# Last layer of a graph network: gathered rows turned ahead of made rows on TensorE, VectorE's step in another order

## What is computed

```python
x = concatenate([nodes[senders], nodes[receivers], edges], axis=-1)
h = relu(x @ msg_W1 + msg_b1)
messages = relu(h @ msg_W2 + msg_b2)
agg = segment_sum(messages, receivers, num_segments=3125)
y = relu(concatenate([nodes, agg], axis=-1) @ node_W1 + node_b1)
y = y @ node_W2 + node_b2
y = (y - mean(y)) * rsqrt(var(y) + 1e-5) * ln_scale + ln_offset
return nodes + y
```

## Time and profile before

| | |
|---|---|
| median of 3 runs | 1332.59 us (1330.99 to 1334.54) |
| the profiled execution | 1327.6 us, its span 1325.8 us |
| busy, share of the span | PE 76%, DVE 63%, POOL 45%, ACT 34% |
| last layer's loop and what surrounds it | about 716 to 1326 us |

### The profile page before, as it was taken

How to read it: one execution, slowest core, us unless ns; L and a number is a source line. 1 busy time by engine, 2 the same in 40 slices (tenths; PEclk the granted TensorE clock), 3 DMA queues, 4 the chain that set the end, 5 groups by cost and what they waited for, 6 DMA issues and landing times.

```text
span 1325.8 us, 24512 instructions
## 1 busy us (share of the span) xinstructions
PE 1006.6 (76%) x6145; PEld 618.1 (47%) x6145; DVE 830.9 (63%) x2605; ACT 452.6 (34%) x1035; POOL 592.2 (45%) x763
## 2 busy tenths in 40 slices
PE   3788887996667767667696787777787878777685
PEld 2566553553444545445355444434444534444443
DVE  8988877357645556757657554565555555555556
ACT  3677771011434333334013232232232323222232
POOL 6533330000665666654003656555555555555550
PEclk9677778998887788877797899999888998999997
DMA  2000006001111111100523533333333333333331
GB/s 54 2 0 0 0 0 243 1 1 22 24 23 19 20 21 22 21 19 17 168 63 75 138 81 79 76 76 76 77 73 77 75 71 77 75 73 78 72 75 34
DMA packets 145110, 72.80 MB, mean 55 GB/s; under 512 B 111917, under 2 KB 136698, under 8 KB 144922
## 3 DMA queue, kind: packets, MB, share of 16 engines
q1 hardware_dynamic: 127224, 54.98, 16.0%
q0 software_dynamic: 16448, 16.88, 6.9%
q10 hardware_dynamic: 1378, 0.22, 0.1%
HBM read 59.66 MB, written 12.35 MB: 54 GB/s over the span
## 4 chain that ended last, share of the span: by engine, by line
PE 41%; another core or an unknown queue 20%; issue 16%; DVE 12%; ACT 6%; DVEq 2%; POOL 1%; ACTq 1%; DMA 1%; SPq 1%; POOLq 0%
PE seg L1628 10%; PE big L1658 5%; PE big L1552 4%; PE seg L1683 4%; PE seg L1755 3%; PE big L1791 3%; PE seg L1802 2%; ACT A L1345 2%; PE seg L1566 2%; PE big L1781 1%; ACT A L1466 1%; PE seg L1696 1%; ACT A L1472 1%; PE seg L1823 1%
## 5 line engine op out<-in xcount | busy, mean ns | idle before, releaser
L1221 POOL DMA_INDIRECT A<-table,idx x338 | 327.3, 968 | 260.6 <-ACT idx L1317 154.2
L1221 POOL DMA_INDIRECT pair<-table,idx x176 | 176.2, 1001 | 126.8 <-ACT idx L1317 65.0
L1755 PE MATMUL seg<-A 128*128 128x384 f16 (+1 forms) x624 | 137.6, 370 | 44.5 <-issue 19.1
L1466 ACT COPY A<-big 128x512 f32<-128x512 f32 x104 | 61.1, 587 | 249.7 <-remote 156.7
L1345 ACT CAST A<-big 128x500 f32 x208 | 125.4, 603 | 48.0 <-PE big L1557 25.9
L1791 PE MATMUL big<-A 128*128 128x512 f32 x208 | 114.1, 631 | 33.6 <-ACT A L1466 28.3
L2033 DVE COPY A<-seg 128x512 f32<-128x512 f32 x52 | 36.0, 691 | 162.3 <-remote 150.6
L1683 PE MATMUL seg<-A,cur 128*64 128x160 f32 x750 | 94.8, 353 | 46.0 <-issue 45.9
L1397 ACT COPY A<-big 128x500 f32<-128x500 f32 x120 | 66.5, 576 | 181.4 <-remote 113.8
L1755 PEld LDWEIGHTS seg<-A 128*128 128x128 f16 x624 | 60.3, 106 | 140.5 <-issue 91.0
L1658 PE MATMUL big<-A 128*128 128x300 bf16 x480 | 106.1, 367 | 18.8 <-issue 10.4
(11 more groups left out here) (307 smaller groups left out, 1809.6 us busy)
## 6 DMA issues: line engine op xcount, KB each, us to landing
A<-in_edge_attr_dram SPq DMA_DIRECT2D x103, 128.0 KB
A<-drel_flat SPq DMA_DIRECT2D x104, 126.0 KB
spilled_adjacency<-A SPq DMA_DIRECT2D x1, 7074.0 KB, 21.8
A<-spilled_adjacency SPq DMA_DIRECT2D x6, 1152.0 KB, 11.8
A<-table,idx POOLq DMA_INDIRECT x338
A<-pr_table SPq DMA_DIRECT2D x104, 31.5 KB
pair<-table,idx POOLq DMA_INDIRECT x176
A<-low_flat SPq DMA_DIRECT2D x78, 32.0 KB
```

Of the source, the lines that this page charges most:

```text
L1221: pool.indirect_dma_start(out=row(q, j), out_offset=None, in_=table, in_offset=bass.IndirectOffsetOnAxis(ap=idx[:, q, j:j + 1], axis=0)).t ...
L1466: nc.scalar.copy(x_t[:, r, :], big[:, r, :]).then_inc(x_t_ready[r], 1)
L1755: op = nc.tensor.matmul(made[:, 0:held.shape[2] * D], hot_low[:, u, m, :], held[:, k, :, :], start=(m == 0 and k == 0), stop=(m == 3 and k ...
```

## The change

Three things. On TensorE `turn_rows` of the step's lag-1 group stands ahead of `make_rows`. On VectorE the list begins with `choose_rows` and `add_windows` instead of ending with them. And the six instructions that centre `node_w2` and `node_b2` are no longer ahead of the loop, but at the beginning of step 4; `steps` has a new argument for that.

```diff
-        def steps(eng, stages, between=lambda s: None):
+        def steps(eng, stages, between=lambda s: None, ahead=lambda s: None):
...
             for s in range(peeled * Q):
+                ahead(s)
                 one_step(0, s, 0, GROUPS)
...
-            steps(pe, [(0, make_rows), (1, turn_rows), (0, node_hidden), (6, window_sums), (2, hidden_sums), (4, turn_messages), (3, message_sums)])
+            steps(pe, [(1, turn_rows), (0, make_rows), (0, node_hidden), (6, window_sums), (2, hidden_sums), (4, turn_messages), (3, message_sums)])
...
-            for weights, many in ((nw2_sb, HID), (nb2_bc, P)):
-                link(dve.tensor_reduce(st_a[0:many, 0:1], weights, AX.X, ALU.add))
-                link(dve.tensor_scalar(st_c[0:many, 0:1], st_a[0:many, 0:1], 1.0 / D, None, ALU.mult))
-                link(dve.tensor_scalar(weights, weights, st_c[0:many, 0:1], None, ALU.subtract))
-            dve.sem_inc(ev("node_weights_ready"), 1)
-            steps(dve, [(1, receivers), (5, message), (0, senders), (4, plain_hots), (0, node_norm),
-                        (7, add_windows),
-                        (0, choose_rows)],
-                  between)
+            def centre_weights(s):
+                if s != Q:
+                    return
+                for weights, many in ((nw2_sb, HID), (nb2_bc, P)):
+                    link(dve.tensor_reduce(st_a[0:many, 0:1], weights, AX.X, ALU.add))
+                    link(dve.tensor_scalar(st_c[0:many, 0:1], st_a[0:many, 0:1], 1.0 / D, None, ALU.mult))
+                    link(dve.tensor_scalar(weights, weights, st_c[0:many, 0:1], None, ALU.subtract))
+                dve.sem_inc(ev("node_weights_ready"), 1)
+
+            steps(dve, [(0, choose_rows), (7, add_windows), (1, receivers), (5, message), (0, senders), (4, plain_hots), (0, node_norm)],
+                  between, centre_weights)
```

## The result

The changed kernel takes 1370.45 us (median of 4 runs, 1367.82 to 1373.35) against 1331.79 us (4 runs, 1329.96 to 1334.54) for the kernel before on the same chip: 1.0289 times, 95% interval 1.0261 to 1.0317. It is 39 us slower. The forecast of 1326 us and its range up to 1354 us were wrong, and the time lies in the slower rival's span of 1354 to 1383 us.

What follows compares the result with a forecast made beforehand. GpSimd's timeline (gathers, gaps and waits for index copies) was taken to bound the last layer. The early turn's 6.7 us off 1327.6 gave 1320.9; with 5.0 us from execution to median, 1325.9, say 1326 us, range 1312 to 1354.

Steps and rivals of the forecast that it cites:

- slower rival: VectorE becomes the bound: make_rows(3)'s increment held, choosing only at the release, turn and hidden_sums late; 1354 to 1383 us, chance 0.26.
- VectorE, order: VectorE's list with choose_rows first: make_rows(3) and hidden_sums(1) start 0.7 to 1.2 us later, all hidden, costing nothing.
- cover of 2.4 us: Slack between hidden_sums(1) ending at 1008.30 and its use at 1010.72, claimed to hide the later make_rows(3).
- TensorE, the early turn: turn_rows ahead of make_rows on TensorE: copy_rows(0) done early, hidden starts at the release; 6.7 us gained, 0 to 9.4.
- The copy of q = 0: ScalarE's copy_rows(0), predicted within 2 us of the start of each run of six gathers.
- 25.5 us of L1791's waits: TensorE's 14 waits for ScalarE's late copy, predicted to be nearly gone.
- The 6.7 us: Gain claimed for the early turn: 0.48 us off each of 14 pauses before runs of seven gathers.
- price per pause: 0.48 us (953.77 to 954.25) saved per long GpSimd pause by taking copy_rows from in front of hidden.
- increments at that point are prompt: TensorE's turn ending soon after a run's first gather reaches ScalarE at once, so copy_rows(0) is done by 1014 or so.
- price per microsecond: In the slower rival, each microsecond over the cover costs 21 us, once a round.
- Centring: node_w2 and node_b2 centring moved to step 4: first senders 1.65 us earlier, hidden by pr_table loads; nothing, 1.65 us either way.
- Gathers under VectorE's work: senders moving against GpSimd's gathers: no change taken; at worst 0.49 us for each of 63 senders, 31 us.

Runs made afterwards that it cites:

- e17: Changed kernel with senders directly behind choose_rows in VectorE's list: 1331.01 us, 1.0093 times the kernel before.
- e6: Changed kernel with senders ahead of choose_rows at the head of VectorE's list: 1.0071 times the kernel before.
- e2: Kernel before with only VectorE's list of the change (choose_rows and add_windows first): 1.0026 times the kernel before.
- e1: Kernel before with only TensorE's list of the change (turn_rows ahead of make_rows): 1327.38 us, 1.0072 times the kernel before.
- e5: Changed kernel (both new lists) with the centring left ahead of the loop: 1342.24 us, 1.0179 times the kernel before.
- e9: Kernel before with ScalarE's list reordered so that the index copy stands ahead of hidden: 1316.91 us, 0.9993 times the kernel before.
- e7: The changed kernel unedited, measured again beside other runs: 1.0223 times the kernel before.
- e8: Kernel before with TensorE's list beginning turn_rows, hidden_sums, make_rows: 1361.27 us, 1.0326 times the kernel before.
- e13: Changed kernel with an iota between the gathers of q = 0 and 1 and of q = 2 and 3: 1376.69 us, 1.0347 times the kernel before.
- e3: Kernel before with only the centring of node_w2 and node_b2 moved to step 4: 1.0040 times the kernel before.
- e11: Changed kernel with ScalarE's index copy ahead of hidden: 1349.76 us, 1.0225 times the kernel before.
- e12: Kernel before with an iota between the gathers of q = 0 and 1 and of q = 2 and 3: single run, 1303.99 us against 1319.99.
- e16: Kernel before with an iota only between the gathers of q = 0 and 1: 1327.52 us, 0.9954 times the kernel before.
- e14: Kernel before with an iota between the gathers of q = 0 and 1 and of q = 2 and 3, timed: 1335.25 us, 1.0039 times.
- e18: Kernel before with an iota between the gathers of q = 0 and 1 and ScalarE's index copy ahead of hidden: 1311.16 us, 0.9931 times.

## Why the prediction was wrong, step by step

**The step that failed** is "VectorE, order", and in it: "make_rows(3) starts 0.7 to 1.2 us later ... All this is hidden, so it costs nothing". I worked the new chain out from the release of one half and held it against one cover of 2.4 us. But the piece from the end of a choosing to the next make_rows comes back twice a round: 1.4 us behind q = 1 (939.82 to 941.24) and 2.3 us behind q = 2 (944.48 to 946.78), in the round shown and in the median round from 820 to 1297 us, where it was 0.25 and 0.06 us before (behind q = 3 it is near 6 us in both kernels). With senders second it is 1.2 and 0.8 us (e17), with senders first 0.75 and 0.77 (e6), and more than half of the loss is gone. The step was also costed with make_rows still ahead of the turn. That is what e2 measures: its pieces are as long as the changed kernel's (1.5 and 2.35 us), and they are nearly hidden, 0.3%. **Behind the early turn they aren't**: from e1 (1.0072) to e5 (1.0179) the same list costs 1.1%, some 14 us, where I had put nothing.

**TensorE, the early turn.** The copy of q = 0 came early as forecast, and the 25.5 us of L1791's waits went. The 6.7 us didn't come; e1 lost 9 us (1327.38 against 1318.45). I had costed what the turn no longer stands behind, and not what now stands behind the turn: make_rows and with it the choosing, which waits for a held increment once a round (121.4 us in e1, 110.1 in the changed kernel; neither the kernel before nor e2 has such a wait in this stretch), and then the turn itself, 3.1 us in the round shown. That this wait is the price of the early turn isn't shown: e9, with the turn at its old place, has more of it (150.2 us, 36 times, 820 to 1280 us) and is as fast as the kernel before. The price per pause was wrong too: e9 took `hidden` out of every pause and gained 0.1%, with an interval from 0.3% faster to 0.2% slower. And the rows didn't bear out that increments at that point are prompt: the turn of 1014.18 is over at 1014.79, and its copy_rows starts at 1017.48, 2.7 us later and before the last gather (1019.11) was begun.

**Both together** cost more than their sum (1.8% against 0.7 + 0.3), which the runs show and I didn't consider at all. A chain fits the timelines: choosing, turn, make_rows held behind senders, choosing again, with hidden_sums and so the index copy behind it. That this chain is why the two don't simply add is argued, not shown. What the traces do show is where the time goes. Over the whole loop GpSimd waits for indices 59, 60 and 60 times in the three kernels with both lists and ScalarE's list as it was (changed, e5, e7), and 48 to 51 times in the kernel before, e1, e2, e6 and e17. `hidden` waits 144 to 165 us for a named, late hidden_sums in the first three, and 17 to 63 us in the others. e8 is slow in another way, with 51 waits of 3.7 us each.

**The slower rival** named the place (the increment of make_rows of q = 3, the choosing at the release, turn and hidden_sums behind) and the price (1354 to 1383 us), and had 0.26. In the changed kernel's timeline it is there word for word. As the cause it is half right: shorter runs of gathers (e13) didn't take the loss away, and where `hidden` waits longer than before, it is for a hidden_sums that ends late by itself. Its price per microsecond was taken for the 21 rounds of the stretch, where the loop has 26; at 26 the span would be 1359 to 1395 us, and the measured time lies in that too.

**Centring**: I took nothing, with 1.65 us either way. The start moved by nothing that can be told; e3 gives 0 to 0.8%, e5 beside e7 nothing to 1%, so whether some 5 us belong to it remains open. **Gathers under VectorE's work**: no change was right, 950 ns after 970; the lengthening that the Trainium skill (SBUF — State Buffer, SBUF: two separate sides) would have for senders at the start of a run isn't in the mean here. The reverse is in e13, where senders took 1.6 to 2.2 us, 0.73 being usual, 15 times of 78, each time with the iota of a stop begun inside it. **The tail** of 7.6 us more I hadn't looked at: once no gather is left only the chain of the other engines remains, and it is the longer one; that this makes the 7.6 us was not tried.

Still open: why the changed kernel is 2.9% slower on one chip and 2.2% on another, why the early turn alone costs 0.7%, and what part of the loss the pattern of runs makes by itself (seven, three and three in the round shown). e11, with both lists and ScalarE's new one, has only 51 waits for indices and is still 2.2% slower; there each takes 3.6 us.

## What to carry to other kernels

When a stage moves in a list, cost what will stand behind it, not only what it no longer stands behind; and follow the loop that goes from engine to engine over a single buffer (choose, make, choose) through all its turns in a round before calling a delay hidden. Two edits that each lean on the other's old order must be costed together. A producer of the next item (senders) belongs ahead of the step that waits for the present one.

## What the runs showed of the hardware

Many increments that TensorE makes late in a run of gathers reach other engines only about 2 to 2.7 us after the last gather of that run was begun: make_rows over at 948.31, the last gather begun at 949.27, the choosing started at 952.00. An iota of 1.1 us between two gathers also let them through, 1.9 to 2.0 us after the gather ahead of it was begun, 24 times in e12, and the next gathers didn't stop what had been let go. One such stop in a round made the kernel 0.5% faster (e16), two made it 0.4% slower (e14). With ScalarE's new list as well (e18) it is 0.6% under e9. Not every increment in a run is held: in the run of 941.80 the choosing of q = 2 starts with 0.04 us behind its make_rows (942.76 to 942.80), and ScalarE copies at 945.64 what the turn of 944.78 ended at 945.44, in the fourth gather of the run. Nor does every held one wait for the end of the run: the copy_rows of 1017.48 in the earlier trace rows came 2.7 us late, in the middle of a run. What in the gathers holds them, and from which point of a run on, no run here shows.

VectorE's four one-hot tiles (senders) take 0.73 us, and 1.6 to 2.2 us when the iota on GpSimd begins inside them (e13, 15 times).
